# A gated delta-rule layer and a mixture of experts on one Trainium2 core: the unit leaves a matmul for a VectorE subtraction, and ScalarE sums the squares it makes

## The chip, the cores and the metric

One core of one Trainium2 chip. The time is the device time of one execution in microseconds; three executions of the kernel before took 1451.58, 1452.80 and 1452.94 us, median 1452.8.

## What is computed

The input is x of shape (2, 512, 256): two sequences of 512 tokens. The first half of the program is a linear-attention layer (gated delta rule) with 16 key heads and 32 value heads of 128, the second a layer of 12 experts. Cut to what matters here:

```python
qkvz = x @ W_qkvz                      # per key head: q 128, k 128, v 2 x 128, z 2 x 128
q, k, v = silu(causal_conv4(q, k, v))
q = q * rsqrt(mean(q^2) + eps) / 128 ;  k = k * rsqrt(mean(k^2) + eps) / sqrt(128)
# per value head, token after token:
S = S * exp(g_t) ; delta = (v_t - k_t S) * beta_t ; S = S + k_t^T delta ; o_t = q_t S
xn = o * rsqrt(mean(o^2) + eps) * norm_w
y = layernorm(x + (silu(z) * xn) @ W_out)
out = layernorm(y + experts(y))        # top 3 of 12, H = 256, I = 640
```

## The kernel before

The recurrence is computed in chunks of 128 tokens: 4 chunks of 2 sequences and 2 value heads make 16 units per key head, and within a chunk the token-by-token solve is one triangular system, whose inverse is built on TensorE. One key head is one pass, and the passes overlap: three of them (n, n+1, n+2) are in work at a time.

The work of a head is a list of named steps. A table `ORDER` writes one window of the steady part out by hand: entries (a, step, x) stand for step x of head w + a, and `MIDDLE` repeats it for w = 1 to 12. `FIRST` stands ahead of it and `LAST` behind it, written out alike. Each engine runs through the same list (function `run`) and takes the steps it has a part in, so the table is the order of every in-order queue at once. `BANK` gives each step with a TensorE product its PSUM bank (2 to 7; 0 and 1 belong to the projections); a step may take its bank when the step ahead of it in that bank was freed.

The steps that matter here, in the order in which a head comes to them:

- `proj` t, `tap` t, `silu` t (t in the order 1, 2, 3, 0): TensorE projects into banks 0 and 1 (L532), ScalarE copies them with the last tap's weight (L802), VectorE adds the other three taps, three instructions that wait for each other (L1023), ScalarE applies SiLU (L809). The next `proj` waits for the taps.
- `kk`, `aT`, `unit`, `aH`, `aL`, `st`, `x0`: the matrix A = unit + aT of each unit, in two float16 parts.
- `y`, `p`, `turn` for five levels and two halves: an approximate inverse X0 and its transpose Z0 in float16.
- `res` g (4 units each): TensorE makes A X0 - 1 in PSUM, with the -1 as a third matmul of `minus16` and `ident16` (L640 to L642). ScalarE evacuates its negative as `res0` in float16 (L875), VectorE the rest as `res1` in bfloat16 (L1085).
- `once` g: res0 times Z0 (L651), evacuated by ScalarE (L879). `Z` g: four matmuls per unit into a bank of its own (L660 to L663), evacuated by ScalarE (L883): one step of refinement, Z = Z0 + (res0 + res1) Z0 + res0 res0 Z0.
- `solve` c, `su` c, `pdl` c, `ks` c, `qs` c: the recurrence over the chunks. `solve` gives the deltas, `su` the state's update (VectorE writes `St`, L1102 and L1108), and `ks` c needs `St` of chunk c - 1. `pdl` gives the outputs `oo`.
- `sqo` c: ScalarE squares the outputs of a chunk (L921, 128x512) into `sqo`; `sum` c: VectorE reduces them to `sso` (L1127), and behind the last chunk adds epsilon (L1132); `power`: GpSimd takes the power -1/2; `weigh` g: VectorE multiplies outputs, factor and SiLU(z) (L1143); `high`, `low` split into two float16 parts; `oT` transposes them by DMA into `oT`, which shares its memory with `sqo`; `op` g multiplies by W_out (L733) and VectorE adds to `y` (L1150).
- `split` z, out, qkv: the weights in two float16 parts (L1007, L1013, L1003 on VectorE).

The evacuation of the residual and the wait that guards it read:

```python
        def residual(n, par, g):
            is_full(act, n, ("res", g), ("Z", g, 1))
            do(res0[:, g], quads(at_bank("res", g)), ACT.Copy, scale=-1.0).then_inc(res_high, 1)
```

## Time and profile before

| | |
|---|---|
| median of three executions | 1452.8 us |
| the profiled execution | 1452.13 us, span on the core 1450.4 us |
| busy: TensorE, its weight loads | 1386.4 us (96%), 1114.9 us (77%) |
| busy: VectorE, ScalarE, GpSimd | 1085.8 (75%), 1049.7 (72%), 697.1 us (48%) |
| granted TensorE clock, mean | 0.982 of full speed |
| attention part, steady windows, experts | to 1104 us, 168 to 936 us, from 1104 us |

Busy time is the union of an engine's instructions. An instruction may start before the one ahead of it has ended: the distance between two starts is then shorter than the duration, and it is the distance that adds up along a queue. A number in square brackets behind a row is idle time of that engine just before it, with what ended it.

### The profile page before, as it was taken

What the parts mean: (1) busy time and instruction counts of PE and PEld (TensorE: products, weight loads), DVE (VectorE), ACT (ScalarE), POOL (GpSimd) and SP (SyncE); (2) the same over time, 40 slices, a digit from 0 to 9 for tenths busy, and PEclk for the clock granted to TensorE, in tenths of its full rate; (3) what the DMA queues carried; (4) which work ended last, traced back from release to release, by engine and by line L of the source; (5) the groups of instructions that cost most, each with busy time, mean ns of one, the idle gap of its engine ahead of it and who ended that gap; (6) DMA issues with size and microseconds to landing.
All of it is one profiled execution on the core that took longest, in us unless ns stands there. A gap on an engine that the chain in (4) does not pass through costs nothing.

```text
span 1450.4 us, 36480 instructions
## 1 busy us (share of the span) xinstructions
PE 1386.4 (96%) x14236; PEld 1114.9 (77%) x14236; DVE 1085.8 (75%) x1926; ACT 1049.7 (72%) x2114; POOL 697.1 (48%) x619
## 2 busy tenths in 40 slices
PE   5689999999999999999999999999978999999996
PEld 3568888898888889798888979888865567667676
DVE  5678999999999999999999999998865512213225
ACT  5777887878788787878888887887755465564651
POOL 0545555446564545556454555545315454353440
PEclk8899999999999999999999999999998999999998
DMA  3000202011020211102030110201131112112100
GB/s 118 16 1 2 67 3 58 24 38 38 24 60 2 60 24 38 38 25 59 2 60 18 44 38 24 60 2 39 32 101 39 56 37 73 38 37 73 37 1 29
DMA packets 100992, 55.76 MB, mean 38 GB/s; under 512 B 74572, under 2 KB 93016, under 8 KB 100824
## 3 DMA queue, kind: packets, MB, share of 16 engines
q1 hardware_dynamic: 100824, 53.43, 14.2%
q8 instruction: 116, 1.90, 0.5%
q14 instruction: 52, 0.43, 0.1%
HBM read 35.59 MB, written 1.05 MB: 25 GB/s over the span
## 4 chain that ended last, share of the span: by engine, by line
PE 89%; DVE 5%; ACT 2%; issue 2%; DMA 1%; POOL 0%; SPq 0%; POOLq 0%; DVEq 0%; ACTq 0%
PE bank L532 11%; PE bank L1486 11%; PE bank L1469 11%; PE bank L687 6%; PE bank L733 5%; PE bank L674 5%; PE bank L704 4%; PE bank L722 4%; PE bank L713 3%; PE bank L622 2%; PE bank L614 2%; PE bank L630 2%; PE bank L582 2%; PE bank L558 2%; PE bank L583 2%; DVE con L1023 2%
## 5 line engine op out<-in xcount | busy, mean ns | idle before, releaser
L1023 DVE SCALAR_TENSOR_TENSOR con<-bank,taps,con 128x1022 f32<-128x1022 f32 (+2 forms) x192 | 245.4, 1278 | 19.9 <-ACT con L802 15.3
L1808 POOL TENSOR_TENSOR h<-h 128x512 f16<-128x512 f32 x120 | 142.5, 1192 | 159.7 <-ACT h L1586 147.7
L532 PE MATMUL bank<-x,qkv 128*128 128x512 f16 x768 | 183.5, 390 | 6.5 <-DVE con L1023 6.5
L1179 POOL TENSOR_TENSOR gl<-const_sb,gc 128x512 f16<-128x512 f32 x128 | 129.9, 1040 | 120.3 <-DVE gc L1033 75.2
L1585 ACT ACTIVATE h<-bank,b 128x512 f32<-128x512 f32 x120 | 82.5, 687 | 119.0 <-PE bank L1469 115.8
L1469 PE MATMUL bank<-y,w 128*128 128x512 f16 x720 | 163.2, 386 | 1.7 <-ACT h L1586 1.4
L1486 PE MATMUL bank<-w,h 128*128 128x256 f16 x1440 | 159.9, 273 | 0.0
L1486 PEld LDWEIGHTS bank<-w,h 128*128 128x128 f16 x1440 | 140.9, 98 | 18.4
L532 PEld LDWEIGHTS bank<-x,qkv 128*128 128x128 f16 x768 | 73.4, 100 | 88.5 <-issue 8.7
L1469 PEld LDWEIGHTS bank<-y,w 128*128 128x128 f16 x720 | 70.2, 99 | 90.6 <-ACT h L1586 8.1
L1214 POOL TENSOR_TENSOR oo<-oo 128x512 f16<-128x512 f32 x64 | 74.2, 1170 | 122.0 <-ACT oo L930 122.0
L1081 DVE TENSOR_TENSOR X<-X,bank 128x512 f16<-128x512 f16 x160 | 109.0, 682 | 16.1 <-PE bank L622 14.7
L1399 DVE SCALAR_TENSOR_TENSOR w<-w,w 128x1280 f16<-128x1280 f32 x12 | 17.8, 1490 | 134.1 <-ACT w L1387 134.1
L871 ACT ACTIVATE Z<-bank 128x512 f16<-128x512 f32 x160 | 96.4, 604 | 23.7 <-PE bank L630 23.7
L1072 DVE TENSOR_TENSOR Y<-bank,ymask 128x512 f16<-128x512 f32 x160 | 109.4, 685 | 2.9 <-PE bank L614 2.3
L802 ACT ACTIVATE con<-bank,taps 128x512 f32<-128x512 f32 x128 | 85.4, 687 | 30.8 <-PE bank L532 30.6
L1206 POOL TENSOR_TENSOR kd<-k_tok,gc 128x512 f32<-128x512 f32 x48 | 50.0, 1043 | 112.0 <-PE bank L713 112.0
L733 PE MATMUL bank<-out,sqo 128*128 128x256 f16 x768 | 96.7, 277 | 7.2 <-ACT zs L889 5.5
L1187 POOL TENSOR_TENSOR pT<-kkm,decay 128x512 f32<-128x512 f32 x64 | 88.0, 1376 | 17.4 <-issue 12.8
L1709 DVE SCALAR_TENSOR_TENSOR facc<-bank,gcol,facc 128x256 f32<-128x256 f32 x88 | 38.5, 479 | 76.6 <-PE bank L1486 76.6
L674 PE MATMUL bank<-z,x 128*128 128x256 f16 x768 | 89.6, 273 | 1.4 <-ACT zs L889 0.8
L733 PEld LDWEIGHTS bank<-out,sqo 128*128 128x128 f16 x768 | 73.3, 99 | 22.1 <-issue 8.7
(222 smaller groups left out, 3858.2 us busy)
## 6 DMA issues: line engine op xcount, KB each, us to landing
w<-in_w SPq DMA_DIRECT2D x24, 640.0 KB, 4.4
w_qkv<-in_W_qkvz SPq DMA_DIRECT2D x16, 512.0 KB, 4.3
w_out<-in_W_out SPq DMA_DIRECT2D x16, 256.0 KB, 3.0
w_z<-in_W_qkvz SPq DMA_DIRECT2D x16, 256.0 KB, 2.9
Z<-in_xT SPq DMA_DIRECT2D x2, 512.0 KB, 5.5
y<-in_x SPq DMA_DIRECT2D x1, 1024.0 KB, 7.8
sqo<-oo SPq DMA_TRANSPOSE x64, 2.7
out_dram<-y SPq DMA_DIRECT2D x8, 128.0 KB, 1.8
```

The source lines that it names most:

```text
L532: last = mm(bank[:, b], qkv16[:, w, a, t * P:(t + 1) * P], x16[:, x, a, b * S:(b + 1) * S], start=(a == k == 0), stop=(a == HT - 1 and k = ...
L674: last = mm(out[:, j * 256:(j + 1) * 256], x16[:, x, a, m * P:(m + 1) * P], z16[:, w, a, :], start=(a == k == 0), stop=(a == HT - 1 and k ...
L733: last = mm(out[:, j * H:(j + 1) * H], oT[:, g % 2, o, 2 * j + r], out16[:, w, r, :], start=(r == i == 0), stop=(r == R - 1 and i == len(P ...
L871: freed(do(dst, src, ACT.Copy), "turn", lh)
L1023: stt(out=out, in0=bank[:, 0:B, 0:S - k], scalar=taps[:, par, t, TAPS - 1 - k:TAPS - k], in1=out, op0=ALU.mult, op1=ALU.add).then_inc(tap_ ...
L1072: freed(tt(Y[:, h], at_bank("y", lh).rearrange("p (u k) -> p u k", u=8), ymask[:, l].unsqueeze(1).broadcast_to([P, 8, P // 2]), ALU.mult), ...
L1081: freed(tt(x, x, at_bank("p", lh).rearrange("p (q b) -> p q b", b=b), ALU.subtract), "p", lh)
L1179: last = tt(gl[:, g % 2, k].rearrange("p (m r) d -> p m r d", m=2), upper.unsqueeze(1).unsqueeze(1).broadcast_to([P, 2, R, P]), gc[:, par, ...
L1187: tt(pT[:, par, 4 * g:4 * g + 4].rearrange("p (m r) d -> p m r d", m=2), kkm[:, g % 2, :, 1].unsqueeze(2).broadcast_to([P, 2, R, P]), deca ...
L1469: last = mm(h_bank(n, k), w1_16[:, n % 2, w, a, t * P:(t + 1) * P], y16[:, x, a, h * S:(h + 1) * S], start=(a == i == 0), stop=(a == HT - ...
L1486: last = mm(o_bank(k)[:, j * H:(j + 1) * H], h16[:, n % 2, h, t, m * P:(m + 1) * P], w2_16[:, n % 2, w, t, :], start=(t == i == 0), stop=( ...
L1808: tt(h16[:, n % 2, 1, t, at], h32[:, k % H32], h16[:, n % 2, 0, t, at], ALU.subtract).then_inc(h_low, 1)
```

## The change

Three things, and a table written anew for them.

1. The -1 is no longer a matmul. `res` is two matmuls per unit (A X0). VectorE now evacuates both parts: `res0` = 1 - A X0 in one instruction that multiplies by -1 and adds `ident16`, and `res1` as before from the same bank, which now holds A X0, so `res1` carries a -1. ScalarE has no part in `res` any more.
2. `Z` has no bank of its own. It goes on adding to the bank of `once`, which already holds res0 Z0: three matmuls per unit (res0 times once, res1 times Z0, and `twice16`, twice the unit, times Z0, which makes up for the -1). ScalarE evacuates that bank twice, once as `once` and once as `Z`; new semaphores `once_ready` and `z_full` order this.
3. `sqo` is four ScalarE instructions per chunk of 128 columns, each with `accum_out` into its column of `sso`. Their elementwise output is not used; it goes into `oo16`. VectorE's reductions fall away; only the small instruction that adds epsilon is left at the last `sum`. `oT` gets memory of its own, and its DMA waits for the output products of the step two before it instead of for the sums.

```diff
-    minus16 = sb("minus16", [P, P], F16)
+    twice16 = sb("twice16", [P, P], F16)
+    oT = sb("oT", [P, 2, 2, 4, P], F16)
-    sqo = sb("sqo", [P, 2, B, R, P])
...
             sp.wait_ge(oo_low, 4 * n + g + 1)
-            if g < 2:
-                sp.wait_ge(sum_done, 5 * n + 5)
-            else:
-                is_full(sp, n, ("op", g - 2))
+            is_full(sp, n, ("op", g - 2) if g >= 2 else ("op", g + 2, 1))
...
                 mm(out[:, at], aH[:, u], X0[:, u], start=True, stop=False)
-                mm(out[:, at], aL[:, u], X0[:, u], start=False, stop=False)
-                last = mm(out[:, at], minus16[:], ident16[:], start=False, stop=True)
+                last = mm(out[:, at], aL[:, u], X0[:, u], start=False, stop=True)
...
-            is_free(pe, n, ("res", g), ("once", g), taking=("Z", g))
-            out = take(n, "Z", g)
+            pe.wait_ge(once_ready[g], n + 1)
+            is_free(pe, n, ("res", g))
+            out = at_bank("once", g)
             for j in range(4):
                 u, at = 4 * g + j, slice(j * P, (j + 1) * P)
-                mm(out[:, at], res0[:, g, j], once[:, g % 2, j], start=True, stop=False)
-                mm(out[:, at], res1[:, g, j], Z0[:, u], start=False, stop=False)
-                mm(out[:, at], res0[:, g, j], Z0[:, u], start=False, stop=False)
-                last = mm(out[:, at], ident16[:], Z0[:, u], start=False, stop=True)
-            filled(last, "Z", g)
+                mm(out[:, at], res0[:, g, j], once[:, g % 2, j], start=False, stop=False, skip_group_check=True)
+                mm(out[:, at], res1[:, g, j], Z0[:, u], start=False, stop=False, skip_group_check=True)
+                last = mm(out[:, at], twice16[:], Z0[:, u], start=False, stop=True, skip_group_check=True)
+            last.then_inc(z_full[g], 1)
...
-            if after(n, 1) or c >= 2:
-                act.wait_ge(sum_done, 5 * n + c - 1)
-            if c < 2:
-                is_full(act, n, ("op", 2 + c, 1))
-            last = do(sqo[:, c % 2], oo[:].rearrange("p (b c r) d -> p b c r d", b=B, c=CH)[:, :, c], ACT.Square)
+            if c == 0 and after(n, 1):
+                act.wait_ge(rso_ready, n + 1)
+            if after(n, 1):
+                act.wait_ge(oT_in[c // 2], 16 * n)
+                act.wait_ge(oT_in[2 + c // 2], 16 * n)
+            for b in range(B):
+                for r in range(R):
+                    u = (b * CH + c) * R + r
+                    last = do(oo16[:, u // 4, 0, u % 4], oo[:, u], ACT.Square, accum_out=sso[:, u:u + 1])
...
         def residual(n, par, g):
+            is_full(dve, n, ("res", g))
+            if after(n, 1):
+                dve.wait_ge(z_full[g], n)
+            stt(out=res0[:, g], in0=quads(at_bank("res", g)), scalar=-1.0,
+                in1=ident16[:].unsqueeze(1).broadcast_to([P, 4, P]), op0=ALU.mult, op1=ALU.add).then_inc(res_high, 1)
             dve.wait_ge(res_high, 4 * n + g + 1)
...
         def sum_squares(n, par, c):
-            if c == 0 and after(n, 1):
-                dve.wait_ge(rso_ready, n + 1)
-            dve.wait_ge(sq_out, CH * n + c + 1)
-            nc.vector.tensor_reduce(sso[:].rearrange("p (b c r) -> p b c r", b=B, c=CH)[:, :, c], sqo[:, c % 2],
-                                    AX, ALU.add).then_inc(sum_done, 1)
             if c == CH - 1:
-                dve.wait_ge(sum_done, 5 * n + CH)
+                dve.wait_ge(sq_out, CH * n + CH)
```

The tables `FIRST`, `ORDER`, `LAST` and `BANK` are written anew. In `ORDER` the steps of most engines stand as before but for a few neighbours, as in

```diff
-    (1, "kk", 0), (1, "load", "z"), (1, "aT", 0), (1, "kk", 1),
```

Three places show what it comes to. In the first, VectorE in the steady part, from the weighting of the last two groups of outputs (`weigh 2`, `weigh 3`; `oo<-oo,rso,zs`) to the copy into `St`. Before (`res<-bank,res` is `res1`, `y<-bank,y` the output products' evacuation, `con` the taps):

```order
L1143 SCALAR_TENSOR_TENSOR oo<-oo,rso,zs 128x128 x8
L1085 SCALAR_TENSOR_TENSOR res<-bank,res 128x512
L1150 SCALAR_TENSOR_TENSOR y<-bank,y 128x512
L1023 SCALAR_TENSOR_TENSOR con<-bank,taps,con 128x2x511
L1023 SCALAR_TENSOR_TENSOR con<-bank,taps,con 128x2x510
L1023 SCALAR_TENSOR_TENSOR con<-bank,taps,con 128x2x509
L1085 SCALAR_TENSOR_TENSOR res<-bank,res 128x512
L1150 SCALAR_TENSOR_TENSOR y<-bank,y 128x512
L1085 SCALAR_TENSOR_TENSOR res<-bank,res 128x512
L1150 SCALAR_TENSOR_TENSOR y<-bank,y 128x512 x2
```

The same place now:

```order
L1148 SCALAR_TENSOR_TENSOR oo<-oo,rso,zs 128x128 x8
L1092 SCALAR_TENSOR_TENSOR res<-bank,ident 128x512
L1095 SCALAR_TENSOR_TENSOR res<-bank,res 128x512
L1155 SCALAR_TENSOR_TENSOR y<-bank,y 128x512
L1092 SCALAR_TENSOR_TENSOR res<-bank,ident 128x512
L1095 SCALAR_TENSOR_TENSOR res<-bank,res 128x512
L1028 SCALAR_TENSOR_TENSOR con<-bank,taps,con 128x2x511
L1028 SCALAR_TENSOR_TENSOR con<-bank,taps,con 128x2x510
L1028 SCALAR_TENSOR_TENSOR con<-bank,taps,con 128x2x509
L1155 SCALAR_TENSOR_TENSOR y<-bank,y 128x512
L1092 SCALAR_TENSOR_TENSOR res<-bank,ident 128x512
L1095 SCALAR_TENSOR_TENSOR res<-bank,res 128x512
```

Three of the four new instructions (L1092) stand here, each right ahead of the one that reads it; `res 1` has come ahead of the taps. The stretch goes on, now:

```order
L1155 SCALAR_TENSOR_TENSOR y<-bank,y 128x512 x2
L1059 TENSOR_TENSOR kkm<-bank,const_sb 128x512
L1065 TENSOR_TENSOR aT<-kkm,decay 128x512
L1092 SCALAR_TENSOR_TENSOR res<-bank,ident 128x512
L1095 SCALAR_TENSOR_TENSOR res<-bank,res 128x512
L1059 TENSOR_TENSOR kkm<-bank,const_sb 128x512
L1065 TENSOR_TENSOR aT<-kkm,decay 128x512
L1012 SCALAR_TENSOR_TENSOR z<-w_z,z 128x512
L1018 SCALAR_TENSOR_TENSOR out<-w_out,normw,out 128x512
L1059 TENSOR_TENSOR kkm<-bank,const_sb 128x512
L1071 TENSOR_TENSOR X<-bank,const_sb 128x512
L1112 COPY St<-bank 128x512
```

The fourth pair stands here, before the second `kk` (it stood behind both splits, alone), and all of it stands ahead of the copy into `St`.

The second place is ScalarE around the copy of `proj 2` (L802, now L799). Before, with the squares as `sqo<-oo`:

```order
L851 ACTIVATE decay<-bank,gc 128x128 x4
L921 ACTIVATE sqo<-oo 128x512
L809 ACT_TABLE_LOAD
L809 ACTIVATE con<-con 128x1024
L921 ACTIVATE sqo<-oo 128x512
L871 ACTIVATE Z<-bank 128x64x8
L802 ACTIVATE con<-bank,taps 128x512 x2
```

Now, with the squares as `oo,sso<-oo`:

```order
L848 ACTIVATE decay<-bank,gc 128x128 x4
L926 ACTIVATE oo,sso<-oo 128x128 x4
L806 ACT_TABLE_LOAD
L806 ACTIVATE con<-con 128x1024
L926 ACTIVATE oo,sso<-oo 128x128 x4
L871 ACTIVATE Z<-bank 128x64x8
L799 ACTIVATE con<-bank,taps 128x512 x2
```

The order is the same; one instruction became four in two places.

The third place is TensorE at the start of head 15's recurrence, where `solve 0` is `bank<-v_tok,Z` and an output product `op` is the row of 12. Before:

```order
L704 MATMUL bank<-v_tok,Z 128x128 x4
L733 MATMUL bank<-out,sqo 128x256 x12
L713 MATMUL bank<-dl,kd 128x128 x4
L722 MATMUL bank<-dl,pT 128x128 x4
L687 MATMUL bank<-St,kT 128x256 x2
```

Now:

```order
L730 MATMUL bank<-out,oT 128x256 x12
L701 MATMUL bank<-v_tok,Z 128x128 x4
L637 MATMUL bank<-X,aH 128x128
L638 MATMUL bank<-X,aL 128x128
...
L710 MATMUL bank<-dl,kd 128x128 x4
L647 MATMUL bank<-Z,res 128x128 x4
L730 MATMUL bank<-out,oT 128x256 x12
L684 MATMUL bank<-St,kT 128x256 x2
```

Before, one output product (`op 3`) stood behind `solve 0`; now two do (`op 2` here, and `op 3` further on), and so does `res 3`.

## Rows read from the trace of the kernel before

**Rows 1.** The page: busy time by engine, and the chain by engine.

```profile
PE 1386.4 (96%) x14236; PEld 1114.9 (77%) x14236; DVE 1085.8 (75%) x1926; ACT 1049.7 (72%) x2114; POOL 697.1 (48%) x619
...
PE 89%; DVE 5%; ACT 2%; issue 2%; DMA 1%; POOL 0%; SPq 0%; POOLq 0%; DVEq 0%; ACTq 0%
```

**Rows 2.** Busy time by stretch: from:to, length, then each engine (instructions), clock, DMA.

```profile
589.44:653.34 63.90, 63.78 (x746) 54.74 (x744) 59.73 (x105) 52.51 (x114) 34.13 (x31) 1.00 0.14 35
1000.00:1010.00 10.00, 10.00 (x115) 9.53 (x114) 7.12 (x11) 6.24 (x17) 7.43 (x8) 1.00 0.01 2
```

**Rows 3.** Timeline of VectorE in one steady period: start us, length us, instruction, [idle before].

```profile
592.78 3.90 DVE L1023 SCALAR_TENSOR_TENSOR con<-bank,taps,con 128x1022 f32<-128x1022 f32 x3
...
601.10 3.90 DVE L1023 SCALAR_TENSOR_TENSOR con<-bank,taps,con 128x1022 f32<-128x1022 f32 x3
604.91 2.18 DVE L1143 SCALAR_TENSOR_TENSOR oo<-oo,rso,zs 128x128 f32<-128x128 f32 x8
607.61 0.69 DVE L1085 SCALAR_TENSOR_TENSOR res<-bank,res 128x512 bf16<-128x512 f32 x1 [0.52 <-ACT res L875]
608.22 0.68 DVE L1150 SCALAR_TENSOR_TENSOR y<-bank,y 128x512 f32<-128x512 f32 x1
609.29 3.91 DVE L1023 SCALAR_TENSOR_TENSOR con<-bank,taps,con 128x1022 f32<-128x1022 f32 x3 [0.39 <-ACT con L802]
...
616.35 0.69 DVE L1054 TENSOR_TENSOR kkm<-bank,const_sb 128x512 f32<-128x512 f32 x1 [0.16 <-PE bank L583]
617.07 0.69 DVE L1060 TENSOR_TENSOR aT<-kkm,decay 128x512 f32<-128x512 f32 x1
...
623.64 0.69 DVE L1102 COPY St<-bank 128x512 f32<-128x512 f32 x1 [0.25 <-PE bank L713]
```

**Rows 4.** Timeline of TensorE: `proj 2` and `ks 1` of the same period.

```profile
589.07 2.76 PE L532 MATMUL bank<-x,qkv 128*128 128x512 f16 x12
...
625.04 1.03 PE L687 MATMUL bank<-St,kT 128*128 128x256 f32 x4
```

**Rows 5.** Timeline of TensorE: first matmul of a `res` group, and what follows its twelve.

```profile
603.62 0.22 PE L640 MATMUL bank<-X,aH 128*128 128x128 f16 x1
...
604.29 1.47 PE L733 MATMUL bank<-out,sqo 128*128 128x256 f16 x12
```

**Rows 6.** Groups by line and form, 200 to 900 us: busy us, mean ns, idle before.

```profile
L1085 DVE SCALAR_TENSOR_TENSOR res<-bank,res 128x512 bf16<-128x512 f32 x44 | 30.1, 683 | 5.7 <-ACT res L875 5.7
...
L1127 DVE TENSOR_REDUCE sso<-sqo 128x4 f32<-128x512 f32 x42 | 26.7, 678 | 0.0
```

**Rows 7.** Timeline of ScalarE around the copy of `proj 2`.

```profile
587.07 0.67 ACT L921 ACTIVATE sqo<-oo 128x512 f32<-128x512 f32 x1
587.76 1.28 ACT L809 ACT_TABLE_LOAD   x1
589.05 1.06 ACT L809 ACTIVATE con<-con 128x1024 f32<-128x1024 f32 x1
590.24 0.63 ACT L921 ACTIVATE sqo<-oo 128x512 f32<-128x512 f32 x1
590.77 0.58 ACT L871 ACTIVATE Z<-bank 128x512 f16<-128x512 f32 x1
591.25 1.30 ACT L802 ACTIVATE con<-bank,taps 128x512 f32<-128x512 f32 x2
592.65 0.28 ACT L824 ACTIVATE sq<-bank 128x128 f32<-128x128 f32 x1
592.82 0.19 ACT L824 ACTIVATION_READ_ACCUMULATOR sq<-bank 128x1 f32 x1
...
594.66 0.65 ACT L871 ACTIVATE Z<-bank 128x512 f16<-128x512 f32 x1
```

**Rows 8.** Timeline of TensorE: an output product in head 15's part.

```profile
1054.28 1.47 PE L733 MATMUL bank<-out,sqo 128*128 128x256 f16 x12
```

More of the change, by code:

```diff
@@ new lines @@
+    (13, "sqo", 3), (14, "turn", (2, 1)), (13, "sum", 3), (14, "norm", 0),
+    (15, "proj", 2), (14, "p", (3, 1)), (13, "power", 0), (15, "sq1", 1),
+    (15, "tap", 2), (13, "weigh", 0), (15, "tok", 0), (15, "tok", 1),
+    (13, "z", 0), (14, "y", (4, 1)), (13, "weigh", 1), (15, "silu", 2),
+    (13, "z", 1), (13, "high", 0), (13, "z", 2), (14, "turn", (3, 1)),
+    (15, "proj", 3), (14, "p", (4, 1)), (15, "tap", 3), (13, "high", 1),
+    (15, "v", (0, 1)), (14, "turn", (4, 0)), (13, "low", 0), (15, "kT", 0),
```

235 lines of the change are left out of this document (128 added, 107 removed), and 237 rows, old and new, of tables (BANK, FIRST, LAST, ORDER).

## The prediction

> **What bounds the kernel now.** I read the page's chain first, then the stretches by engine, then the timelines. The chain that ended last runs through TensorE (PE) for 89% of the span, and PE is busy 96% of it [rows 1]. One period of the steady part shows it more sharply: 63.9 us per head, PE busy 63.78 of them, VectorE (DVE) 59.73, ScalarE (ACT) 52.51 [rows 2]. There are 12 such periods, one for each w of `MIDDLE`. PE saves time only if whatever feeds it keeps up, and DVE has only 4.2 us of air per period. So the question is where that air lies.
>
> The timeline of DVE answers it [rows 3]. From the first tap of step `tap 2` at 592.78 to the weighting that starts at 604.91 no row has a wait (eight groups, of which three stand here); behind it the row of `res` waits 0.52, the next tap step 0.39, `kkm` 0.16 and the copy into `St` 0.25. That copy (623.64 to 624.33) is what PE's `ks 1` at 625.04 needs [rows 3, 4]. Call the stretch from `tap 2` to `ks 1` the dense one. The rest of the period, from `ks 1` round to the next `proj 2`, is PE without a gap (625.04 to the next 652.97, which is 589.07 and a period) [rows 4].
>
> **What PE loses.** `res` falls from 3 matmuls per unit to 2, `Z` from 4 to 3: 32 of 128x128 fewer per head, 512 in all. Twelve of them run from 603.62 to 604.29 [rows 5], 0.056 each, so a head saves 1.8 us and the kernel 28.6 us, if PE is what ends it. But 28 of the 32 lie inside the dense stretch; only `Z 3` (4 x 0.056 = 0.22) lies behind `ks 1`.
>
> **What DVE gains and loses.** It loses four reductions per head (678 ns) and takes on four new instructions of the kind of L1085 (683 ns) [rows 6]: busy time hardly moves. The place moves. The reductions lay in pairs before `tap 1` and before `tap 2`; all four new instructions lie in the dense stretch, as the order shows. Each is followed by the instruction that reads its result and waits for it. Bounds for such a step: 0.61 between the starts of two that don't need each other (607.61 to 608.22), 0.72 where the second reads the first (616.35 to 617.07) [rows 3]. I take 0.72, since the new pair is of the second kind: 4 x 0.72 = 2.88 us. The waits there give way: 0.52 + 0.39 + 0.16 + 0.25 = 1.32, and each wait also costs the 0.08 by which neighbours overlap otherwise (683 ns long, 0.60 apart), 1.64 in all. Net: `St` comes 1.24 later.
>
> The Trainium skill ("VectorE: DVE Perf Modes", section "The DRAIN you can't avoid") says that a semaphore between two DVE operations costs nothing extra. By it the new step would cost what an independent one costs, 0.11 less, and the sum would be some 5 us less (48 x 0.11); the two pairs of rows above differ by just this, so the trace does not bear it out.
>
> **What the freed place before `tap 2` is worth.** Nothing, I think. `tap 2` needs ACT's copy of `proj 2`, which ends at 592.55 (591.25 + 1.30), and DVE started at 592.78 [rows 3, 7]. Without the reductions DVE only waits there for ACT.
>
> **What ACT gains and loses.** It loses four evacuations of `res` (0.5 us each in starts) in a stretch where it has air. Its four squares of 512 columns become sixteen of 128 with an accumulator read each. One of 512 takes 0.53 from start to start (590.24 to 590.77); eight with the read take 2.01 (592.65 to 594.66), 0.25 each, so four cost 1.00 [rows 7]. The other end is no overlap at all: 0.28 and 0.19 of the read, 1.88 for four. I take 1.00, the row of the same function and width; it reads from PSUM, the new ones from SBUF. Over the head the sum is about even, but again the place counts: `sqo 2` and `sqo 3` stand on ACT just ahead of the copy of `proj 2`, with the table load and the SiLU between them. They make it 2 x 0.47 = 0.94 later. Of this 0.13 was a wait before 590.24 and 0.18 the gap between 592.55 and 592.78: `tap 2` starts 0.6 later, and no DVE wait up to 604.91 takes this back.
>
> The Trainium skill (same page, section "The TRN2 errata — SBUF-src ops pay a fixed extra latency per instruction") speaks against cutting a ScalarE operation up: every instruction that reads SBUF pays again, and it gives 293 ns against 250 ns for 128 columns from PSUM. As an estimate from that page, the eight squares ahead of `tap 2` cost 0.35 more, some 4 us in all. No row here has a narrow square from SBUF.
>
> **The sum.** `St` late by 0.6 + 2.88 - 1.64 = 1.84. PE's slack on it was 0.71 (624.33 to 625.04), of which I leave 0.06 for the handover: `ks 1` is 1.19 late, `Z 3` gives 0.22 back, the period grows by 0.97 to some 64.9 us. Twelve of them: +11.6 us. In `LAST` it goes the other way: from 1000 to 1010 DVE has 2.9 of 10 us free and PE none [rows 2], so head 14's matmuls count there (about 1.5 us); the split of `out` leaves the dense stretch (1.0); and `op 2` now stands behind `solve 0` of head 15, where PE waits on the recurrence anyway, one group of 1.3 us [rows 8]. I take -4, bounds 0 and -6. In `FIRST` the taps and ACT set the pace before PE does; I take 0, bounds ±2. `twice16` and the bank of `Z` that is no longer taken cost nothing; the transposes of the outputs no longer wait for the sums, which were over anyway: the `low` part that they wait for comes behind them through `power` and `weigh`. The experts' part is untouched. Against the profiled execution: 1452.1 + 11.6 - 4 = 1459.7 us. The median of the runs is 0.7 above that execution, so **1460.4 us**. A measurement can tell 0.2% (2.9 us) from no change.
>
> **Rivals.**
> *PE keeps its saving.* If the copy into `St` came in time, the period would be 63.9 - 1.8 = 62.1: 12 x 1.8 = 21.6 and the 4 of the end, 1427 us. For it: PE is 99.8% busy, and DVE's total (59.73 and four times the 0.11 by which 0.72 exceeds 0.61, some 60.2) still fits under 62.1. Against it: the order leaves the two splits and all four pairs between `tap 0` and `St`, while DVE's air lies elsewhere. 10%.
> *Cheap steps.* This ends faster. The place is again the copy into `St`; the period shrinks if the delay of `tap 2` and the four new instructions together stay under 1.64 + 0.65 + 0.22 = 2.51 us. With 0.61 per new step (607.61 to 608.22) they are 2.44, and if `tap 2` is not late at all, the period is 0.1 shorter: -1 and -4, so 1447.8 us. For it: both kinds of step are the same instruction, and only the wait differs. Against it: the pair at 616.35 [rows 3], and a ScalarE that hardly rests here [rows 7]. 15%. The rule on the DRAIN, cited above, points this way.
> *Only DVE's part is real.* ACT's squares find cover, `tap 2` starts as before: +0.37 per period, 4.4, and -4: 1453 us, no change that can be told. For it: ACT rests for 11 us of each period [rows 2]. Against it: it waits hardly between `solve 3` and the copy. 17%.
> *My forecast*, with dearer squares as its upper side (1.88 for four would add 1.8 per period and reach 1481), 58%.
>
> **Range and chances.** The low end, 1446, takes in the cheap steps and leaves out the first rival. The high end, 1470, goes half of the way to unoverlapped squares. Faster: 10 + 15 = 25%. Same: 17%. Slower: 58%.
>
> **What would show it.** A steady period near 64.9 us with PE busy about 62 of it; PE's weight load of `ks 1` or the solve behind it waiting for DVE's `St`; no DVE wait between `weigh 2` and `St`; DVE waiting up to 1.5 us for ACT's copy before `tap 2`; ACT squares 0.25 apart; a tail (from the last `proj` on) some 3 us shorter. A period below 63.5 would refute the argument; one of 64.3 with `tap 2` on time would mean that only ACT's term was wrong.

## The result, and the profile after

| | before | after |
|---|---|---|
| median (lowest to highest) | 1452.6 us (1451.6 to 1452.9, four executions) | 1484.0 us (1480.3 to 1485.5, four) |
| the profiled execution, its span | 1452.1, 1450.4 us | 1485.5, 1483.7 us |
| granted TensorE clock, mean | 0.982 | 0.979 |

The ratio is 1.0214, with a 95% interval of 1.0196 to 1.0233: slower by 2.1%, as forecast in sign, and 14 us above the top of the range. The page of the changed kernel, busy time and the chain by engine (for [rows 1]):

```profile
PE 1372.2 (92%) x13724; PEld 1087.5 (73%) x13724; DVE 1096.4 (74%) x1926; ACT 1053.8 (71%) x2498; POOL 691.5 (47%) x619
...
PE 63%; DVE 17%; ACT 11%; issue 7%; POOL 1%; DMA 1%; DVEq 0%; POOLq 0%; ACTq 0%; SPq 0%
```

TensorE has 512 matmuls fewer and is 14 us less busy, yet the chain runs through it for 63% only, where it was 89%. VectorE and ScalarE now stand in the chain. The chain is the row of steps that ended last, each followed back to what released it. To see where the time goes, take one instruction per head as a milestone, VectorE's copy of the gates (`gc`). Before, for heads 2 and 14:

```profile
133.41 0.21 DVE L1033 COPY gc<-gates 128x96 f32<-128x96 f32 x1
...
901.82 0.21 DVE L1033 COPY gc<-gates 128x96 f32<-128x96 f32 x1
```

The same two after:

```profile
141.29 0.21 DVE L1038 COPY gc<-gates 128x96 f32<-128x96 f32 x1
...
932.42 0.21 DVE L1038 COPY gc<-gates 128x96 f32<-128x96 f32 x1
```

Of the 33.3 us between the two spans, 7.9 lie ahead of head 2's copy, 22.7 between the two (twelve periods, 64.03 before and 65.93 after on average, 1.90 more each), and 2.7 behind. The prediction had 0, 11.6 and -4.

A period of the changed kernel, by engine (for [rows 2], same columns), and what TensorE waits for in 200 to 900 us: who waits, at which line, for whom; us in total, times, longest. The kernel before has no row in this second view.

```profile
602.79:668.72 65.93, 62.82 (x714) 52.87 (x713) 60.67 (x105) 52.74 (x137) 33.62 (x30) 1.00 0.13 34
```

```profile
PE bank L611 <- ACT Z L871: 10.4, 11, 0.9
PE bank L730 <- ACT Z L884: 8.6, 11, 0.8
PE bank L619 <- issue: 7.3, 11, 0.7
PE bank L701 <- DVE kkm L1059: 4.1, 10, 0.4
PE bank L671 <- DVE X L1086: 3.4, 11, 0.3
```

Five waits, 33.8 us in eleven periods or 3.1 us in each, and 65.93 less 62.82 busy is 3.1: the profile of one period and the list of waits say the same. The largest is `y (4, 1)` (L611). The second is `op 2` (L730), waiting for bank 2, which `once 0` and `Z 0` now hold together. The third is `p (3, 1)` (L619); "issue" means that the profile names nobody for it. The fourth is `solve 0` (L701), whose bank VectorE frees with its mask of `kk 1`, and the last stands at a `z` (L671). In TensorE's timeline the first and the third are

```profile
613.25 0.39 PE L619 MATMUL bank<-Y,Z 128*128 128x64 f16 x8 [0.66 <-issue]
...
617.04 0.39 PE L611 MATMUL bank<-X,aH 128*128 128x64 f16 x8 [0.94 <-ACT Z L871]
```

and ScalarE's timeline shows what they wait for (its accumulator reads left out):

```profile
612.29 0.29 ACT L926 ACTIVATE oo<-oo 128x128 f16<-128x128 f32 x1
...
612.58 0.57 ACT L871 ACTIVATE Z<-bank 128x512 f16<-128x512 f32 x1
613.06 1.24 ACT L799 ACTIVATE con<-bank,taps 128x512 f32<-128x512 f32 x2
...
616.25 0.65 ACT L871 ACTIVATE Z<-bank 128x512 f16<-128x512 f32 x1
```

The evacuation of `turn (2, 1)` (612.58) stands behind the last of the new squares, and `p (3, 1)` starts 0.67 after it. That of `turn (4, 0)` (616.25) stands behind the eight squares of the keys, and `y (4, 1)` starts 0.79 after it. Before, `y (4, 1)` came behind `z 2`, when this had long been done. The new table has it between `z 0` and `z 1`.

VectorE after, from the wait before `tap 2` to `St` (compare [rows 3]):

```profile
612.71 0.17 DVE L1137 SCALAR_TENSOR_TENSOR sso<-sso,epsw 128x16 f32<-128x16 f32 x1 [1.15 <-ACT oo L926]
...
613.69 0.69 DVE L1086 TENSOR_TENSOR X<-X,bank 128x512 f16<-128x512 f16 x1 [0.73 <-PE bank L619]
614.34 3.91 DVE L1028 SCALAR_TENSOR_TENSOR con<-bank,taps,con 128x1022 f32<-128x1022 f32 x3
...
623.75 3.90 DVE L1028 SCALAR_TENSOR_TENSOR con<-bank,taps,con 128x1022 f32<-128x1022 f32 x3
...
629.67 0.69 DVE L1092 SCALAR_TENSOR_TENSOR res<-bank,ident 128x512 f16<-128x512 f32 x1
630.39 0.69 DVE L1095 SCALAR_TENSOR_TENSOR res<-bank,res 128x512 bf16<-128x512 f32 x1
...
643.83 0.68 DVE L1012 SCALAR_TENSOR_TENSOR z<-w_z,z 128x512 f16<-128x512 f32 x1
644.43 1.12 DVE L1018 SCALAR_TENSOR_TENSOR out<-w_out,normw,out 128x512 f16<-128x512 f32 x1
...
646.77 0.69 DVE L1112 COPY St<-bank 128x512 f32<-128x512 f32 x1
```

Count from the gate copy. `tap 2` came 10.75 us behind it before (592.78 less 582.03) and comes 11.55 behind it now (614.34 less 602.79). `tap 3` followed `tap 2` after 8.32 and now after 9.41: here `y (4, 1)` sits. `St` followed `tap 3` after 22.54 and now after 23.02. The rest of the period, from `St` to the next gate copy, was 22.29 and is 21.95 now.

### The profile page after: what moved, and what is told of

It reads as the page before. It is cut to its first block, busy times and chain, and to the rows that moved or that the text cites. A ratio compares the mean times of both kernels' runs of the same rounds, so it can differ in the third digit from the quotient of the medians.

```text
span 1483.7 us, 35898 instructions
## 1 busy us (share of the span) xinstructions
PE 1372.2 (92%) x13724; PEld 1087.5 (73%) x13724; DVE 1096.4 (74%) x1926; ACT 1053.8 (71%) x2498; POOL 691.5 (47%) x619
## 4 chain that ended last, share of the span: by engine, by line
PE 63%; DVE 17%; ACT 11%; issue 7%; POOL 1%; DMA 1%; DVEq 0%; POOLq 0%; ACTq 0%; SPq 0%
PE bank L1491 11%; PE bank L1474 10%; PE bank L529 7%; PE bank L684 6%; DVE con L1028 6%; PE bank L701 4%; PE bank L719 3%; PE bank L710 3%; PE bank L671 3%; ACT oo L926 2%; PE bank L611 2%; DVE res L1092 2%; PE bank L619 2%; DVE y L1155 2%; DVE oo L1148 2%
## 5 line engine op out<-in xcount | busy, mean ns | idle before, releaser
L799 ACT ACTIVATE con<-bank,taps 128x512 f32<-128x512 f32 x128 | 86.1, 685 | 46.7 <-PE bank L529 46.3
L730 PE MATMUL bank<-out,oT 128*128 128x256 f16 x768 | 96.1, 276 | 19.1 <-ACT Z L884 9.7
L730 PEld LDWEIGHTS bank<-out,oT 128*128 128x128 f16 x768 | 73.5, 99 | 34.5 <-issue 18.4
L671 PE MATMUL bank<-z,x 128*128 128x256 f16 x768 | 91.5, 273 | 5.2 <-DVE X L1086 3.8
```

The lines of the kernel that those rows point to most:

```text
L671: last = mm(out[:, j * 256:(j + 1) * 256], x16[:, x, a, m * P:(m + 1) * P], z16[:, w, a, :], start=(a == k == 0), stop=(a == HT - 1 and k ...
L730: last = mm(out[:, j * H:(j + 1) * H], oT[:, g % 2, o, 2 * j + r], out16[:, w, r, :], start=(r == i == 0), stop=(r == R - 1 and i == len(P ...
```

## The experiments

All kernels of this section were timed in three rounds beside the kernel before, except where a row has more executions; medians of the kernel before lay between 1452.1 and 1453.3. "Head 2" is the start of its gate copy, "period" the mean of the twelve between the copies of heads 2 and 14, "rest" the span behind the latter, all from the one profiled execution of each kernel. "Head 2" moves by over 2 us with the list `FIRST` unchanged (140.0 in e3, 137.8 in e6), so single differences of that size say nothing there.

| kernel | us | ratio, 95% interval | head 2 | period | rest |
|---|---|---|---|---|---|
| before | 1452.6 | | 133.4 | 64.03 | 548.6 |
| after | 1484.0 | 1.0214 (1.0196 to 1.0233) | 141.3 | 65.93 | 551.3 |
| e1 | 1548.4 | 1.0663 (1.0647 to 1.0679) | 138.9 | 71.15 | 554.2 |
| e2 | 1469.6 | 1.0119 (1.0102 to 1.0137) | 140.3 | 64.93 | 548.1 |
| e3 | 1471.9 | 1.0135 (1.0118 to 1.0151) | 140.0 | 65.18 | 547.1 |
| e4 | 1464.8 | 1.0087 (1.0072 to 1.0102) | 133.3 | 64.98 | 550.8 |
| e5 | 1459.4 | 1.0050 (1.0033 to 1.0066) | 140.1 | 64.15 | 548.4 |
| e6 | 1456.7 | 1.0036 (1.0021 to 1.0051) | 137.8 | 64.17 | 546.2 |
| e7 | 1504.4 | 1.0357 (1.0337 to 1.0376) | 138.7 | 67.43 | 551.1 |
| e8 | 1493.6 | 1.0290 (1.0273 to 1.0307) | 133.5 | 67.22 | 551.6 |
| e9 | 1459.6 | 1.0047 (1.0032 to 1.0062) | 137.8 | 64.16 | 548.1 |
| e10 | 1459.7 | 1.0046 (1.0031 to 1.0061) | 133.7 | 64.63 | 548.6 |
| e11 | 1478.3 | 1.0183 (1.0165 to 1.0200) | 147.6 | 64.97 | 547.0 |
| e15 | 1462.0 | 1.0069 (1.0052 to 1.0086) | 140.3 | 64.23 | 549.6 |
| e16 | 1469.1 | 1.0112 (1.0096 to 1.0128) | 140.3 | 64.86 | 548.9 |
| e17 | 1469.4 | 1.0110 (1.0089 to 1.0131) | 140.9 | 64.90 | 550.2 |
| e18 | 1471.7 | 1.0136 (1.0118 to 1.0154) | 138.7 | 64.92 | 551.1 |
| e19 | 1458.1 | 1.0038 (1.0026 to 1.0050) | 135.5 | 64.17 | 548.3 |
| e20 | 1458.8 | 1.0042 (1.0028 to 1.0056) | 136.4 | 64.26 | 548.9 |
| e21 | 1469.3 | 1.0108 (1.0089 to 1.0128) | 136.1 | 65.07 | 551.0 |

### First: which part costs what (e1 to e4)

**e1**, the changed instructions in the old `ORDER`:

```diff
-    (0, "res", 3), (1, "kk", 1), (1, "aT", 1), (0, "split", "z"),
-    (0, "split", "out"), (0, "Z", 2), (0, "once", 1), (1, "aH", 0),
+    (1, "kk", 1), (1, "aT", 1), (0, "split", "z"), (0, "split", "out"),
+    (0, "Z", 2), (0, "once", 1), (0, "res", 3), (1, "aH", 0),
...
-    (1, "res", 1), (2, "proj", 0), (1, "once", 0), (2, "tap", 0),
-    (0, "op", 1), (1, "res", 2), (0, "low", 2), (0, "low", 3),
...
+    (2, "proj", 0), (1, "once", 0), (2, "tap", 0), (1, "res", 1),
+    (0, "op", 1), (0, "low", 2), (0, "low", 3), (1, "res", 2),
```

> The changed kernel with the steady window's order of the kernel before (new operations, new FIRST, LAST and banks). Theory A (the new order is part of the cost: y of level 4, second quarter, now stands between z 0 and z 1 on TensorE and waits there for ScalarE's evacuation behind the eight squares of the keys, 0.94 us, plus 0.66 around it): the period falls by about 1.1 us, 12 periods, 13 us, so about 1471 us. Theory B (all of the cost is in the operations): within 2 us of 1484.

It missed by 77 us, for a reason of its own. Some of TensorE's and VectorE's waits, 200 to 900 us (L590 is `st`, a step at the start of the inverse):

```profile
DVE y L1155 <- PE bank L730: 44.7, 20, 2.5
...
PE bank L647 <- DVE res L1092: 41.5, 10, 4.2
...
PE bank L590 <- DVE res L1095: 15.1, 10, 1.5
```

`once 2` needs VectorE's new `res0` of `res 2`. In the old order this stands behind the three taps of `tap 0` and behind `res 1`, and TensorE waits 4.2 us for it in each period. ScalarE, which made `res0` before, had no taps in its queue. So some of the new order is needed by the change itself; the run says nothing of the forecast's terms.

**e2**, one entry of the new `ORDER` back in its old place:

```diff
-    (0, "z", 0), (1, "y", (4, 1)), (0, "z", 1), (2, "silu", 2),
-    (0, "high", 0), (0, "z", 2), (0, "low", 0), (0, "low", 1),
+    (0, "z", 0), (0, "z", 1), (2, "silu", 2), (0, "high", 0),
+    (0, "z", 2), (1, "y", (4, 1)), (0, "low", 0), (0, "low", 1),
```

> The changed kernel with one entry of the window moved back: y of level 4 and half 1 behind z 2. Theory A: this entry is nearly all of the order's cost, so as the run with the whole old order, about 1472 us, and no row of TensorE waits for ScalarE between z 0 and z 1. Theory B: about 1484. If the old order helps and this does not, the cost lies in another entry.

That entry costs 1.00 us per period and 14.4 us in all. With it back, one period in the middle is 64.83 us (595.3 to 660.1), where the forecast had 64.87. That is in part luck, for the growth is made up otherwise than forecast: e6, below, leaves 0.13 for the residual's change, where the forecast had 0.37.

**e3** is the change of the residual and of `Z` alone, with `sqo` and VectorE's reductions as before (and `y (4, 1)` in the changed kernel's place). **e4** is the kernel before with the change of `sqo` alone:

```diff
-            last = do(sqo[:, c % 2], oo[:].rearrange("p (b c r) d -> p b c r d", b=B, c=CH)[:, :, c], ACT.Square)
+            for b in range(B):
+                for r in range(R):
+                    u = (b * CH + c) * R + r
+                    last = do(oo16[:, u // 4, 0, u % 4], oo[:, u], ACT.Square, accum_out=sso[:, u:u + 1])
```

In e3, against the changed kernel:

```diff
-                    last = do(oo16[:, u // 4, 0, u % 4], oo[:, u], ACT.Square, accum_out=sso[:, u:u + 1])
+            last = do(sqo[:, c % 2], oo[:].rearrange("p (b c r) d -> p b c r d", b=B, c=CH)[:, :, c], ACT.Square)
...
+            nc.vector.tensor_reduce(sso[:].rearrange("p (b c r) -> p b c r", b=B, c=CH)[:, :, c], sqo[:, c % 2],
+                                    AX, ALU.add).then_inc(sum_done, 1)
```

> The changed kernel with the squares undone: one square of 512 columns on ScalarE and VectorE's reductions again; the residual's change and the new order stay. Theory A (the squares hold ScalarE's copy of proj 2 up by 0.6 us per head, VectorE only waits where the reductions stood): 12 x 0.6 = 7 us less than the changed kernel, about 1477 us. Rival (VectorE is what bounds, and every 0.6 us reduction that comes back costs its time): up to 12 x 2.4 = 29 us more, about 1510 us.

> The kernel before with the squares' change alone (sixteen squares of 128 columns with accumulation, no reductions, its own memory for oT), its own order and banks. Theory A (tap 2 comes 0.6 us late; the waits of 1.6 us further on take most of it up): 0 to 0.3 us per period, 1453 to 1457 us. Rival (TensorE is paced by the chain proj, copy, tap, so 0.6 us late stays 0.6 us late): +7.5, about 1460 us.

Taking the squares away gives 0.75 per period; adding them alone to the kernel before costs 0.95. Here e4's theory missed. The four reductions that VectorE is rid of buy nothing, and it is not only `tap 2` that is late. TensorE itself waits, and the kernel before has no such row (e4, the largest of its waits, 200 to 900 us; L618 is `p`):

```profile
PE bank L618 <- issue: 7.4, 11, 0.7
```

### Second: the squares placed (e5, e6)

**e5** is e2 with two entries moved, so that `squares 2` run while ScalarE waits anyway, and the evacuation of `turn (2, 1)` goes ahead of the squares. **e6** is e3 with `y (4, 1)` back, so the residual's change alone.

```diff
-    (1, "y", (2, 1)), (1, "turn", (1, 1)), (1, "p", (3, 0)), (2, "gc", 0),
...
-    (0, "sum", 2), (0, "sum", 3), (0, "sqo", 2), (0, "oT", 2),
-    (2, "silu", 1), (0, "sqo", 3), (1, "turn", (2, 1)), (1, "norm", 0),
+    (1, "y", (2, 1)), (1, "turn", (1, 1)), (0, "sqo", 2), (1, "p", (3, 0)),
...
+    (1, "p", (4, 0)), (0, "sum", 2), (0, "sum", 3), (0, "oT", 2),
+    (1, "turn", (2, 1)), (2, "silu", 1), (0, "sqo", 3), (1, "norm", 0),
```

> The changed kernel with y (4, 1) back behind z 2 (as in the run before this one), and with two steps of ScalarE moved in ORDER: squares 2 in front of p (3, 0) and turn (2, 1) in front of silu 1. Theory (the eight squares cost time only because they stand ahead of turn (2, 1)'s evacuation and of proj 2's copy): the squares' 0.8 us per period go, the period falls from 64.8 to some 64.0 and the time from 1469.6 to 1460 (1456 to 1463). Rival (ScalarE's added 2 us per head count wherever they stand): no change, 1468 to 1471.

> The change to the residual and Z alone (sums of squares as before), with y (4, 1) back behind z 2. Theory (the three costs add: squares 0.8, place of y (4, 1) 1.1, residual 0.1 us per period): period 64.0, time 1472 less 13 = 1459 (1456 to 1462), so slower than before by what the new FIRST costs, though TensorE has 32 matmuls fewer per head. Rival (the place of y (4, 1) costs only together with the squares, which stand ahead of the evacuation it waits for): 1468 to 1472.

Both came as expected: 64.15 and 64.17. In e5 the wait at L619 is gone, and with it the squares' 0.8 us per period. (That moving `turn (2, 1)` and `sqo 2` would gain nothing without the new squares was not run.) The costs of the steady part are 1.00 for `y (4, 1)` (after less e2), 0.76 for the squares (e2 less e6) and 0.13 for the residual's change (e6 less before). These three must add up to the 1.89 lost, since they are differences along one row of kernels; the check is e3, which gives 1.01 for `y (4, 1)` without the squares and 0.75 for the squares, and e4, which gives 0.95 for the squares alone. And 0.13 is the surprise: TensorE has 32 matmuls less to do per head there, 1.8 us by the forecast, and the period is no shorter. Its main waits in e6 (L735 is the output product, L706 `solve`, L676 `z`):

```profile
PE bank L735 <- ACT Z L889: 7.8, 10, 0.8
PE bank L706 <- DVE kkm L1060: 4.4, 11, 0.4
PE bank L676 <- DVE X L1087: 3.7, 11, 0.3
```

That is 1.5 us per period, and e5, which has the same three waits, shows the same by its busy time, 64.00 less 62.50 (590.02 to 654.02). Of the forecast's 1.8 us of saving the busy time shows 1.28 (63.78 less 62.50):

```profile
590.02:654.02 64.00, 62.50 (x714) 52.98 (x713) 59.69 (x106) 52.94 (x138) 33.61 (x30) 1.00 0.13 35
```

### Third: what eats TensorE's saving (e7 to e10, e15 to e18, e20, e21)

My theory was the prediction's: VectorE's stretch from `tap 2` to `St` sets the period. So its work was to be taken out of that stretch. **e7** moves the splits of `z` and `out` on both engines to behind the gate copy; **e8** does the same to the kernel before. **e9** and **e10** leave ScalarE's halves where they were (as a step `cut`) and move VectorE's alone:

```diff
-    (0, "res", 3), (1, "kk", 1), (1, "aT", 1), (0, "split", "z"),
-    (0, "split", "out"), (0, "Z", 2), (0, "once", 1), (1, "aH", 0),
...
+    (1, "kk", 1), (1, "aT", 1), (0, "cut", "z"), (0, "cut", "out"),
...
+    (0, "split", "z"), (1, "load", "z"), (0, "sum", 0), (0, "sum", 1),
...
+    (1, "p", (4, 0)), (0, "sum", 2), (0, "split", "out"), (1, "load", "out"),
```

> The run with the squares placed, and also the splits of z and out moved from the dense stretch of VectorE (between res 3 and St) to behind the gate copy, where VectorE waits; the next load of z behind them. Theory (what eats TensorE's saved 1.8 us per head is that VectorE runs without a wait from tap 3 to St, so 1.3 to 1.8 us taken out of that stretch come back at each period): period 62.3 to 62.9, time 1438 to 1447. Rival (TensorE is held elsewhere): under 3 us less than the run with the squares placed.

> The kernel before with the same move of the two splits and of the load. Theory: before, TensorE was the bound of that stretch and VectorE waited 1.6 us in it, so the move gives nothing by itself: 1449 to 1454. Rival (the dense stretch held the kernel before as well): 1435 to 1445.

> The run with the squares placed, with only VectorE's halves of the splits of z and out moved (ScalarE's stay where they were, as a step of their own, so that VectorE never waits for them): z behind the gate copy, where VectorE waits 1.7 us before tap 1, out in front of the sum of squares before tap 2, where it waits 1.1 us; the loads behind them. Theory (the stretch of VectorE without waits from tap 2 to St sets the period): 1.65 us come out of it, period 62.3 to 62.9, time 1439 to 1447. Rival (TensorE is held elsewhere, and the splits in the waits push tap 1 and tap 2 back): 1456 or more.

> The kernel before with the same move of VectorE's two halves. Theory: before, TensorE was as much the bound (busy 63.78 of 63.90 us), VectorE had 1.6 us of waits in the stretch, so nothing is gained: 1450 to 1455. Rival (VectorE's stretch was the bound of the kernel before too): 1432 to 1445.

e7 and e8 failed by placement: the splits stood on ScalarE ahead of the copy of `proj 1`, VectorE waited 1.47 us for them (e7, L1012 at 611.13, shown in the last section), and `tap 1` was late. e9 has no such fault, and gained nothing: the period is 64.16, where e5 has 64.15. VectorE's freed time turned into waiting inside the very stretch (e9, VectorE's waits; L1072 masks `X`, behind `kk 2`):

```profile
DVE X L1072 <- PE bank L591: 19.7, 22, 1.3
```

while TensorE's three waits stayed. So that end of the stretch, where the splits were and where the prediction saw the handover at `St`, sets nothing in this version. The kernel before lost 0.6 per period by the same move (e10). There TensorE's output products wait for the transposes of the outputs, 0.4 us per period; why these come late was not followed up (L734 is the output product; `sqo` shares its memory with `oT`):

```profile
PE bank L734 <- DMA sqo<-oo: 4.7, 7, 1.1
```

**e15** exchanges banks, to free `op 2` of its wait. **e16** puts `res 3` behind `aT 1`, to mask `kk 1` sooner, which frees the bank of `solve 0`; **e17** does both to e6.

```diff
-    ("kk", 0): 6, ("kk", 1): 4, ("once", 1): 6, ("res", 3): 2, ("kk", 2): 5,
+    ("kk", 0): 6, ("kk", 1): 4, ("once", 1): 6, ("res", 3): 3, ("kk", 2): 5,
...
-    ("op", 1): 6, ("res", 2): 4, ("once", 2): 3, ("op", 2): 2, ("decay", 1): 5,
+    ("op", 1): 6, ("res", 2): 4, ("once", 2): 2, ("op", 2): 3, ("decay", 1): 5,
```

> The run with the squares placed (1459.4, period 64.00), with three banks exchanged: op 2 and res 3 on bank 3, once 2 on bank 2. Theory (of the 1.5 us by which the period is longer than TensorE's 62.50 busy, 0.78 are op 2 waiting for bank 2, which once 0 and Z 0 now hold together until ScalarE's copy of Z 0): that wait goes, period 63.2, time 1450 (1448 to 1453). Rival (VectorE's stretch behind tap 2 sets the period, so the wait turns up again elsewhere): 1457 to 1460.

> As the run before it, and res 3 behind aT 1 (VectorE then frees bank 4, which solve 0 waits for, 1.3 us earlier). Theory: the 0.41 us of solve 0 goes too, period 62.8, time 1445 (1442 to 1449). Rival (res 3 that late makes once 3 or st 0 wait, or VectorE's stretch binds): 1450 or more.

> The residual and Z change alone, y (4, 1) behind z 2 (1456.7, period 64.0), with the same exchange of banks and res 3 behind aT 1. Theory: the same two waits go, period 62.8, time 1442 (1439 to 1446), faster than the kernel before by 0.5 to 1 per cent. Rival: 1452 or more, since VectorE is busier here (61.9 of 64.0 us) than with the squares on ScalarE.

The wait at `op 2` went, and its time came back: 64.23, where e5 has 64.15. TensorE's waits in e15:

```profile
PE bank L701 <- DVE kkm L1059: 4.3, 11, 0.4
PE bank L730 <- DMA oT<-oo: 3.7, 3, 1.6
PE bank L647 <- DVE res L1092: 3.7, 8, 0.5
PE bank L671 <- DVE X L1086: 3.4, 11, 0.3
```

TensorE runs ahead to `once 2` and waits for the new VectorE instruction of `res 2` (L1092), which stands behind the taps; three times it also waits for the transposes. In e16 the wait at `solve` went and a longer one came at `st` (L590), which takes the bank of `kk 2` and so waits for VectorE's mask of it, now behind the pair of `res 3`:

```profile
PE bank L590 <- DVE kkm L1059: 11.6, 11, 1.1
```

e17 fares alike: 64.90, where e6 has 64.17.

**e18** takes one addition of VectorE (0.6 us, that of `op 3`) from in front of `kk 0` to behind `aT 1`. **e20** has this together with e9's splits and e19's list (below), **e21** the banks and two more moves besides.

```diff
+    (0, "res", 3), (1, "kk", 1), (1, "aT", 1), (-1, "add", 3),
```

> The run with the squares placed, with one 0.6 us addition of VectorE, that of op 3 onto the output, taken out of the stretch between tap 2 and kk 1 and put behind aT 1 (TensorE's op 3 stays where it is; its bank 7 is next taken by decay 2). Theory (that stretch of VectorE, up to the mask of kk 1 that frees bank 4 for solve 0, sets the period): kk 1's mask comes 0.6 us earlier, solve 0's wait of 0.41 us goes, period 63.6, time 1454 (1451 to 1456). Rival (another wait takes its place): 1458 or more.

> VectorE's halves of the splits moved out as in e9, and also op 3's addition behind aT 1 as in e18 (in the last list in its old place), with the first half of FIRST in the old order as in e19. Theory (VectorE's stretch holds TensorE at two places one behind the other, at kk 1's mask and at kk 2's, so that e9 and e18, which each shortened it for one of them, gained nothing): with both shorter the period falls to 63.6, the gate copy of head 2 comes at 134 to 136, time 1453 (1450 to 1456). Rival (a third place holds, or kk 1's products on TensorE): period 64.0 or more, 1457 or more.

> As the run before it, and the exchange of banks of e15, op 1's addition behind res 2, and res 3 behind aT 1. Theory (every wait of TensorE that the new sharing of banks and the new VectorE step brought is then taken away together: 0.8 at op 2, 0.4 at once 2, 0.4 at solve 0): period 62.6 to 63.2, time 1442 to 1449, under the kernel before. Rival (what is left of VectorE's stretch holds TensorE again): period 63.6 or more, 1452 or more.

e18 is slower: the period grows by 0.8. The addition now delays the mask of `kk 2`, and TensorE waits 0.5 for it at `st`; and some 3 us are lost in `LAST`, where it stood behind `aT 1` too. e20 was to be the proof, and the rival held: 64.26, where e19 has 64.17. `solve`'s wait fell from 0.4 to 0.2, a new one of 0.2 came for the bank that the late addition holds (L577 is `decay`):

```profile
PE bank L738 <- ACT Z L892: 8.6, 11, 0.8
PE bank L679 <- DVE X L1094: 3.4, 11, 0.3
PE bank L577 <- DVE y L1163: 2.2, 11, 0.2
PE bank L709 <- DVE kkm L1067: 1.7, 11, 0.2
```

In e21 that same bank costs 1.1 us per period, since `op 3`'s addition is later still, and `kk 0` waits another 0.8 for the addition of `op 1`, moved as well:

```profile
PE bank L577 <- DVE y L1163: 12.5, 11, 1.1
PE bank L587 <- DVE y L1163: 9.1, 9, 1.0
```

What these runs show together: TensorE's wait per period is 1.4 us or more in every version of the changed kernel, at three or four handovers, and none of the moves tried took one away without another coming or growing. What they don't show is that VectorE's stretch is the cause: e9 and e20 gave VectorE 1 to 2 us of air in it, and the period stayed at 64.16 and 64.26. Another reading is a loop through ScalarE: the chains of e9 and e20 pass through `silu 1`, the squares, the copy of `proj 2`, the squares of the keys, GpSimd's power of their sums and `tok`. Against the new squares as a needed part of it stands e6, which has none and the same period. No run shortened this loop by itself. What eats TensorE's saving stays open.

### Fourth: the time in front of the steady part (e11, e19)

The four kernels with the old `FIRST` (before, e4, e8, e10) reach head 2 at 133.3 to 133.8; the twelve with the whole new one reach it at 137.8 to 141.3. **e11** puts the old `FIRST` into e5, mended for the shared banks. **e19** puts in only its first 102 steps, and `GATE_BANKS = (4, 2)` as before.

```diff
-GATE_BANKS = (3, 2)
+GATE_BANKS = (4, 2)
-    (0, "load", "qkv"), (0, "split", "qkv"), (0, "tap", 1), (0, "tap", 2),
+    (0, "load", "qkv"), (0, "split", "qkv"), (0, "tap", 1), (0, "proj", 1),
...
```

> The run with the squares placed (1459.4), with the list FIRST of the kernel before in place of the new one, mended where the shared banks ask for it (res 3 behind res 2, Z 2 in front of kT 1, turn (4, 1) in front of once 0). Theory (the 6.7 us that the first three heads lost against before lie in the new order of FIRST, not in the changed instructions): the gate copy of head 2 comes at 133 to 135 instead of 140, time 1452 to 1455. Rival (the heads' first steps lose the time to the added work of VectorE and ScalarE in whatever order): 1458 or more.

> The run with the squares placed, with the first 102 steps of FIRST (head 0, and head 1 up to squares 1) in the order of the kernel before and the gates' two banks as before, the rest of FIRST in the new order. Theory (of the 6.7 us lost up to the gate copy of head 2, 1.8 lie in the new order of head 0 and most of the rest in that of head 1's projections and taps): gate copy of head 1 at 31.5 instead of 33.1 us behind that of head 0, of head 2 at 134 to 136, time 1453 to 1456. Rival (the loss is behind those steps, where res and once follow one another as in the steady part): 1457 or more.

e11 fell into e1's trap: one `once` waits 6.0 us for VectorE's part of `res`, behind the taps, and TensorE also waits 1.2 us for bank 3, which `GATE_BANKS = (3, 2)` keeps until the gates are read. e19 has neither. The gate copies of heads 1 and 2:

```profile
70.71 0.20 DVE L1038 COPY gc<-gates 128x96 f32<-128x96 f32 x1
135.53 0.20 DVE L1038 COPY gc<-gates 128x96 f32<-128x96 f32 x1
```

31.6 us from head 0 to 1 (39.1 to 70.7), as in the kernel before (31.5), where e5 has 33.1. Head 2 comes at 135.5, and at 136.4 and 136.1 in e20 and e21, which have the same list. So these first steps account for a part of the delay, 1.4 to 5.8 us by these two groups, and at least 1.7 us remain behind them. The total shows less: the medians of e19 and e5 differ by 1.3 us (1458.1 and 1459.4), and their intervals overlap.

A rival to the order is the granted clock, and no run separates the two. From 40 to 80 us and from 80 to 133 us its mean was 0.93 and 0.97 in the kernel before, 0.81 and 0.90 in the changed kernel, 0.83 and 0.90 in e5, 0.92 and 0.97 in e19. With the new order TensorE thus runs longer at the lower of its two levels there, which may be a cause of the late head 2 or go along with it. From 200 us to 900 us the mean was 1.00 in the kernel before and in the changed one. No version here beats the kernel before; the nearest are e6 (the change of the residual alone, in a mended table) and e19.

## Why the prediction was right or wrong

- **The sign** was right: slower, because TensorE's saving doesn't reach the end and ScalarE's squares come in the way. That is not luck, for with the entry back that the prediction overlooked (e2) the kernel is still slower by 1.2%. The place where the saving is lost is not the one forecast.
- **The new VectorE step at 0.72** was right to the hundredth: 629.67 to 630.39. The Trainium skill ("VectorE: DVE Perf Modes", section "The DRAIN you can't avoid") says that a semaphore between two VectorE instructions costs nothing extra. By that the step would be the 0.61 of an independent one, such as 630.39 to 631.00, and the trace does not agree. **No wait from `weigh 2` to `St`** was right.
- **The step that failed is the handover at `St`** as the only place where the dense stretch passes its delay on to TensorE: "PE's slack on it was 0.71 [...]: `ks 1` is 1.19 late". From the start of `proj 2` to that of `ks 1` it was 35.97 us before (589.07 to 625.04 [rows 4]) and is 38.34 now, 2.37 more. But from the start of `su 0`, whose product the copy into `St` reads, to the start of `ks 1` it was 2.55 us and is 2.55 now. Before:

```profile
622.49 1.11 PE L713 MATMUL bank<-dl,kd 128*128 128x128 f32 x8
```

  And after:

```profile
609.83 2.76 PE L529 MATMUL bank<-x,qkv 128*128 128x512 f16 x12
...
645.62 1.11 PE L710 MATMUL bank<-dl,kd 128*128 128x128 f32 x8
...
648.17 1.03 PE L684 MATMUL bank<-St,kT 128*128 128x256 f32 x4
```

  The copy started 0.04 behind the end of `su 0` in both, and no list of TensorE's waits of 200 to 900 us has a row for `ks`. The copy waits for TensorE and not TensorE for it. What TensorE waits for are the five handovers ahead of it, 3.1 us, of which the prediction has none: two for ScalarE behind squares (0.94 and 0.66), one for the bank of `Z 0` (0.78), and two for VectorE (0.41 at `solve 0`, 0.31 at a `z`).
- **"The rest of the period, from `ks 1` round to the next `proj 2`, is PE without a gap"** was right: it got 0.34 shorter (27.93 to 27.59), where the forecast had 0.22.
- **The freed place before `tap 2` is worth nothing**: right. VectorE waits 1.15 and 0.73 us there.
- **The squares at 0.25 each** [rows 7]: 0.29 (eight of them from 597.99 to 600.33, 2.34). The Trainium skill (same page, section "The TRN2 errata — SBUF-src ops pay a fixed extra latency per instruction") asks more for a read from SBUF, by an estimate from its table 43 ns for 128 columns on ScalarE, and the trace agrees: 0.29 against the 0.25 of [rows 7]. I had used its figure for no term.
- **`tap 2` starts 0.6 later**: 0.80, 11.55 behind the gate copy against 10.75. The step "no DVE wait up to 604.91 takes this back" looked at VectorE only. The same squares stand ahead of `turn (2, 1)`'s evacuation, and TensorE's `p (3, 1)` waits 0.66 for it, in front of `tap 2`, where the prediction looked for no wait of TensorE. The squares' part of the forecast was 0.6 per period, and 0.75 to 0.95 was measured, in part on another path: e5, which moved both, has neither the wait nor the cost.
- **"Net: `St` comes 1.24 later"** failed. From `tap 3` to `St` it was 0.48. The new steps cost what was forecast, but two neighbours became cheaper: `aT` and the split of `z` took 0.61 and 0.60 from start to start where they had taken 0.96 and 1.04, 0.79 together (see the last section). With this term at 0.48 and everything else as argued, the period would have been 64.1; but by the handover above, a later `St` cost TensorE nothing in any case.
- **The term that is missing by most is that of `y (4, 1)`.** The sum treats `ORDER` as unchanged but for `res`, `Z` and the squares. On TensorE `y (4, 1)` had moved ahead of `z 1` and `z 2`, 1.00 us per period, 14 us in all by e2. The new table says so (`(0, "z", 0), (1, "y", (4, 1)), (0, "z", 1)`); no step of the sum asks what each moved entry waits for.
- **"`twice16` and the bank of `Z` that is no longer taken cost nothing"** left out that `once 0` holds its bank longer: `op 2` waits 0.8 per period for it. What it cost in the end is not shown, since without that wait (e15) the period was no shorter.
- **"PE busy about 62"** of a period: 62.82, and 62.50 in e5. The saving of 1.8 shows as 0.96 and 1.28.
- **`FIRST` "0, bounds ±2"** measured +7.9. I had priced the new instructions there and not the new list, nor the clock. **`LAST` "-4, bounds 0 and -6"** measured +2.7, for all that lies behind head 14's gate copy. In e6, with neither the new squares nor `y (4, 1)` in its new place, it is -2.4.
- **The rivals**: none came true. "Only DVE's part is real" is nearest to what e5 and e6 show once the order is mended (period +0.1, and 4 to 7 us in all), but the kernel as given is not that.

So the 33.3 us between the spans are 7.9 (`FIRST`), 12.0 (`y (4, 1)`, steady part), 9.2 (squares), 1.6 (residual) and 2.7 (`LAST`), differences of the profiled executions. The prediction has the first two at nothing.

## What to carry to other kernels

When a change comes with a table or schedule written anew, compare the two orders on each engine entry by entry, and price every entry that changed neighbours: here one moved entry that the change did not need made 12.0 of the 33.3 us lost, and another 9.2 was where the new squares were put; what the new order of the first steps cost is known less well. Ask of work added to an in-order engine which evacuations stand behind it, and follow each of them to the engine that waits, not only the one that you were looking at. And where an accumulation group is stretched over two evacuations to save matmuls, its bank is held longer: look who takes that bank next. And a wait in the list is not a gain to be had: e15 took away one of 0.8 us per period, and the time came back at other waits.
